# A graph layer on one core: 20 rounds of four gathered units instead of 18 rounds of five

## What is computed

```python
h = x @ node_w.T
rf = edge_attr @ review_w.T
m = (h[src] + rf) * edge_weight
y = segment_sum(m, dst, num_segments=12500)
out = layernorm(x + y, axis=-1)
```

## Time and profile before

| | before |
|---|---|
| median of three runs | 2291.5 us |
| the profiled execution, its own time | 2279.48 us |
| its span | 2277.7 us |
| PE busy, share of the span | 1891.5 us, 83% |
| DVE busy | 1986.1 us, 87% |
| ACT busy | 962.4 us, 42% |
| POOL busy | 1674.5 us, 74% |
| granted TensorE clock, mean | 0.915 |

### The profile page before, as it was taken

How to read it: one execution, slowest core, us unless ns; L and a number is a source line. 1 busy time by engine, 2 the same in 40 slices (tenths; PEclk the granted TensorE clock), 3 DMA queues, 4 the chain that set the end, 5 groups by cost and what they waited for, 6 DMA issues and landing times.

```text
span 2277.7 us, 93210 instructions
## 1 busy us (share of the span) xinstructions
PE 1891.5 (83%) x35999; PEld 1641.8 (72%) x36000; DVE 1986.1 (87%) x6206; ACT 962.4 (42%) x1602; POOL 1674.5 (74%) x1539
## 2 busy tenths in 40 slices
PE   1659788979897989898998899789988998989974
PEld 1557677767776777777777778677777877877864
DVE  3969898989898989898998899889988998989974
ACT  0324344444344444444443445344434443444434
POOL 3777777777777777777777777777777777777700
PEclk8679998999898999999998999899988998989997
DMA  6224333433333333333333333333433333433302
GB/s 139 55 59 86 72 79 79 83 72 83 78 74 76 84 77 84 76 84 77 84 76 76 76 85 80 75 72 84 84 75 69 82 79 71 84 73 72 66 3 57
DMA packets 480104, 173.08 MB, mean 76 GB/s; under 512 B 443549, under 2 KB 455397, under 8 KB 479445
## 3 DMA queue, kind: packets, MB, share of 16 engines
q1 hardware_dynamic: 426791, 111.57, 22.8%
q0 software_dynamic: 49632, 51.95, 11.4%
q10 hardware_dynamic: 3218, 3.20, 0.7%
HBM read 163.39 MB, written 3.20 MB: 73 GB/s over the span
## 4 chain that ended last, share of the span: by engine, by line
POOL 67%; issue 20%; DVE 7%; PE 2%; DMA 1%; ACT 1%; DVEq 0%; POOLq 0%; ACTq 0%; SPq 0%
POOL rows L534 64%; DVE hot_lo L855 3%; DVE hot_key L854 2%; DMA counts<-dst 1%; POOL run_src L560 1%; POOL run_dst L560 1%; POOL run_w L560 1%; POOL dst_row L552 1%; PE x_ps L1438 1%; ACT x_tab L1308 1%; DMA dst_row<-dst,row_i 0%; PE count_ps L1425 0%; DVE packed L990 0%; PE count_ps L1451 0%; DVE x_tab L1010 0%
## 5 line engine op out<-in xcount | busy, mean ns | idle before, releaser
L534 POOL DMA_INDIRECT rows<-x,g_src_cols x1440 | 1584.3, 1100 | 443.6 <-issue 438.7
L1240 ACT ACTIVATE counts<-count_ps 128x588 f32<-128x588 f32 (+1 forms) x1192 | 851.9, 750 | 1138.3 <-PE count_ps L1425 1127.5
L1425 PE MATMUL count_ps<-hot_key,hot_lo 128*128 128x294 f32 x4552 | 897.9, 330 | 257.2 <-DVE hot_lo L855 213.0
L855 DVE SCALAR_TENSOR_TENSOR hot_lo<-count,cols 128x256 fp32r<-128x256 f16 x2276 | 1078.6, 474 | 0.0
L1425 PEld LDWEIGHTS count_ps<-hot_key,hot_lo 128*128 128x128 f32 x4552 | 673.6, 196 | 386.7 <-DVE hot_lo L855 247.5
L854 DVE TENSOR_SCALAR hot_key<-count,cols 128x294 fp32r<-128x294 f16 x2276 | 864.5, 380 | 47.8 <-PE count_ps L1425 27.7
L1438 PE MATMUL x_ps<-counts,x_tab 128*64 128x63 f32 x21364 | 800.2, 229 | 41.3 <-DVE sums L772 41.2
L1438 PEld LDWEIGHTS x_ps<-counts,x_tab 128*64 128x64 f32 x21364 | 725.6, 142 | 102.5 <-DVE sums L772 48.0
L1352 PE MATMUL unit_ps<-rows,g_hot 128*32 128x64 f32 x5760 | 120.8, 246 | 0.0
L1352 PEld LDWEIGHTS unit_ps<-rows,g_hot 128*32 128x32 f32 x5760 | 104.4, 127 | 18.2 <-issue 18.2
L802 DVE TENSOR_SCALAR off<-dst_row,b_all 126x128 f32<-126x128 int32 x18 | 5.2, 290 | 116.4 <-DMA dst_row<-dst,row_i 116.4
(11 more groups left out here) (196 smaller groups left out, 728.3 us busy)
## 6 DMA issues: line engine op xcount, KB each, us to landing
rows<-edge_attr SPq DMA_DIRECT2D x196, 512.0 KB
rows<-x,g_src_cols POOLq DMA_INDIRECT x1440
out<-x_tab SPq DMA_DIRECT2D x12, 256.0 KB
counts<-dst SPq DMA_DIRECT2D x1, 848.0 KB
a_stage<-dst SPq DMA_DIRECT2D x17, 48.0 KB
a_stage_w<-edge_weight SPq DMA_DIRECT2D x17, 48.0 KB
g_stage<-src SPq DMA_DIRECT2D x18, 40.0 KB
g_stage<-dst SPq DMA_DIRECT2D x18, 40.0 KB
```

What stands on the lines that cost most here:

```text
L534: pool.indirect_dma_start(out=g_x[:, i, t, :], out_offset=None, in_=x, in_offset=bass.IndirectOffsetOnAxis(ap=g_src_cols[at.p][:, k:k + 1] ...
L855: dve.scalar_tensor_tensor(hot_lo[h][:, :, :], count16[:, 0:P].unsqueeze(1).to_broadcast([P, 2, P]), cols_[:, LO, j:j + 1], cols_[:, W_LOW ...
L1240: act.activation(to, count_ps[(g + e) % 2][:, 0:n, 0:KEYS].rearrange("p a (h d) -> p a h d", d=D), ACT.Copy).then_inc(counts_read, 1)
L1425: done = pe.matmul(count_ps[(g + e) % 2][:, k % 2, 0:KEYS], hot_lo[h][:, i, :], hot_key[h][:, :], start=(i == 0), stop=(i == 1))
```

## The change

Two constants. All sizes that follow from them change too: 80 gathered units instead of 90, 20 x 378 = 7560 counted nodes instead of 6804, 116 attribute units instead of 106 (of which the last round has two), `rows` with one unit of 4 KB per partition less, and `a_dst` with 116 partitions instead of 106.

```diff
-ROUNDS = 18
-GATHERED = 5
+ROUNDS = 20
+GATHERED = 4
```

## The result

The kernel after takes 2341.32 us in the median of four runs (2336.34 to 2343.08), the kernel before 2289.68 in the runs beside them: 1.0226 times as long, 95% interval 1.0195 to 1.0257. Slower, as forecast. The forecast was 2370, 29 us too high, and the range of 2340 to 2410 holds the time only at its edge, by 1.3 us.

The account below looks back on a forecast made before the run. POOL, saturated by 84 DMAs a round (117.7 us), was taken as the bound, DVE as the next. Two more rounds +115.0, start -31.5, end -4.5 gave +79 us, 2358.5, put on the median as 2370; range 2340 to 2410.

Parts of the forecast that it names:

- POOL's saturation and its end: POOL's DMA queue in the rounds: 84 DMAs, 117.7 us, become 68, 95.3 us; POOL then waits and L802's wait goes.
- What is late next is DVE itself: At L802 in the rounds: the wait goes and DVE sets the pace; POOL's saving beyond 5.6 us a round is worthless.
- DVE per round: DVE's work in a round: 112.1 us left to itself, less 1.1 for the fifth unit, gives 111.0 us.
- The branch, 7.6 us: Loop's branch back, in step 0: 25.2 us with it, 17.6 without; 8 in 18 rounds, the same share as before.
- Rival 2: Steps 4 and 5: PE becomes the bound at its lower clock, 57 us more, 2427 us; chance 14%.
- Rival 1: Rounds: DVE runs faster once not stopped, through L854, branches and slow last steps; 106.6 us a round, 2291 us; chance 5%.
- slow last steps: Part of rival 1: last steps of 18.0 us instead of 16.2, four in 16 rounds, 0.5 us a round, vanish.
- POOL's waits: POOL in the rounds: waits for DVE's row numbers (step 0) and run numbers (end of step 1), together 12 to 17 us.
- The start: Up to the second L802: -31.5 us, 145.76 to 114.3, with -10.2 from a faster a_dst load and fewer gathers ahead.
- rival 3: Start: the a_dst load isn't spread over more engines, L1043 at 27 us, 2382 us; chance 12%.
- The end: After the last L802: -4.5 us from missing fifth units and fewer attribute units in the last round; the tail doesn't change.
- The base: Profile against median: the profiled 2279.5 us lay 12 us below the median, so 2358.5 was lifted to 2370.

Follow-up runs that it names:

- the relief: Kernel before, 18 rounds and five units, with the fifth unit's 16 gathers issued in round 0 only and its other work kept: 2171.66 us, 0.949 times before.
- the renewed load: Kernel after with 16 spare gathers a round into a buffer nobody reads: 2546.03 us, 1.1121 times before.
- the branch experiment: Four rounds in the loop's body instead of two: in the kernel after 2316.43 us, 1.0115 times before; in the kernel before 2289.59 us, 0.9999.
- the run with spare gathers: Kernel after with 16 more gathers a round into a spare buffer nobody reads: 2546.03 us, 1.1121 times before.
- the first experiment: Kernel before with the fifth unit's 16 gathers issued in round 0 only, all other work kept: 2171.66 us, 0.949 times before.
- 90 in the last: 19-round kernel of five and four units in turn, load split, with the fifth unit fetched in its own round behind the next row: 2252.71 us, 0.9834 times before.

## Why the prediction was right, and what was off

**POOL's saturation and its end: right.** No wait at L802 in the rounds, a chain led by DVE, POOL with time left. Both halves show it, the relief (0.949) and the renewed load (1.112), and so does the branch experiment. One word of the prediction is too strong: GpSimd does compute in the set-up (L662, 5.5 us); in the rounds it only issues DMAs.

**"What is late next is DVE itself": right.** DVE is busy for 95.5% of the stretch (forecast: over 93%).

**DVE per round: mis-sized by 0.86 us, 18 x 0.86 = 15.5 us of the 29.** The term that failed is the 112.1 us that "DVE, left to itself, would need". The sum took out the wait at L802 and kept every other idle time and every duration. The run with the fifth unit not fetched measures it: with POOL relieved and DVE's work unchanged a round takes 111.14 us. Of the 1.0 us between, 0.75 is idle time that stood in no row under L802's name (per round, DVE idled 179.9 / 16 = 11.24 us before, 5.57 of it at L802 and 5.67 elsewhere; in that run 4.92 elsewhere), and 0.24 is busy time (106.46 to 106.21). The largest piece of the idle time is the wait for `count_ps` at L854, which fell from 24.7 us to 18.6. The fifth unit's work, forecast at 1.12 us, is 1.0 (111.14 to 110.15), which takes the error back to 0.86.

Why the other waits shrank stays open. It's tempting to call them an echo of the stall: DVE stops, PE runs out of work, the granted clock falls (0.93 in the stretch before, 0.97 with POOL relieved, 0.96 in the kernel after), and DVE waits for the slower PE in turn. But the run with spare gathers speaks against this as a rule. There the stall is back, 177.0 / 18 = 9.8 us a round, and the clock is down to 0.92, yet DVE's idle time elsewhere is (256.4 - 177.0) / 18 = 4.4 us a round, less than the 5.0 of the kernel after, and its waits for `count_ps` are 14.6 us, less than 16.2. The round grew by 9.5 us, 0.3 less than the wait at the row.

**The branch, 7.6 us: right**, and it stayed. DVE's timeline of the kernel after, the ends of steps 5 to 0 and of one whole round; the branch is before the second row:

```profile
1185.12 0.47 DVE L772 TENSOR_TENSOR sums<-sums,x_ps 64x63 f32 x2
1210.10 0.47 DVE L772 TENSOR_TENSOR sums<-sums,x_ps 64x63 f32 x2
1229.16 0.47 DVE L772 TENSOR_TENSOR sums<-sums,x_ps 64x63 f32 x2
1247.24 0.47 DVE L772 TENSOR_TENSOR sums<-sums,x_ps 64x63 f32 x2
1264.58 0.47 DVE L772 TENSOR_TENSOR sums<-sums,x_ps 64x63 f32 x2
1282.83 0.47 DVE L772 TENSOR_TENSOR sums<-sums,x_ps 64x63 f32 x2
1299.03 0.47 DVE L772 TENSOR_TENSOR sums<-sums,x_ps 64x63 f32 x2
1316.66 0.47 DVE L772 TENSOR_TENSOR sums<-sums,x_ps 64x63 f32 x2
```

Step 0 takes 25.0 us with the branch and 17.6 without, as in the earlier trace rows. Step 5 takes 16.2. With five branches fewer, the rounds gave back 6.9 us for each.

**Rival 2, PE as the bound in steps 4 and 5: did not come.** Step 4, without its fifth unit, is 18.2 us, and step 5 is 16.2 in the rows above where the earlier trace rows has a case of 18.0; such cases are gone. The wait that I had read as the cause is still there, in PE's timeline:

```profile
1389.98 1.52 PE L1438 MATMUL x_ps<-counts,x_tab 128*64 128x63 f32 x38 [1.32 <-DVE sums L772]
```

The same 1.32 us as in the earlier trace rows, but the 38 pieces take 1.52 us and not 2.40. So this wait by itself doesn't bring the clock down to 0.50. What does stays open. The stall at L802 isn't shown to: the slow piece begins some 60 us behind it, and the run with spare gathers stops at its row in every round and has no step 5 over 16.9 us.

**Rival 1, a faster DVE: one of its three parts came, at two thirds of its price.** The slow last steps went. The prediction counted four of them in 16 rounds; three lie there (they begin at 1731.77, 1851.51 and 1970.96 us) and the fourth behind, at 2090.23, so they had cost 3 x 1.8 / 16 = 0.34 us a round and not 0.5. L854 didn't move: 863.8 us for 2268 is 0.381, as 767.2 for 2016 was, though a fifth of the DMAs had gone. The branch didn't move.

**POOL's waits: the place was wrong.** I had said 12 to 17 us a round at the row numbers and the run numbers. It is 12.5 in the mean at unit 0 of the next round, for L706; the row is waited for three times in all (21.0 us), the runs hardly, since by then POOL has been held up already. POOL's timeline of the kernel after:

```profile
1199.86 1.09 POOL L552 DMA_INDIRECT dst_row<-dst,row_i  x1 [0.30 <-issue]
...
1218.34 1.01 POOL L534 DMA_INDIRECT rows<-x,g_src_cols  x1 [17.39 <-DVE g_src_cols L706]
```

The time didn't hang on it, but the design does: with 19 rounds, giving POOL something to do in this wait was worth 48 us (2300.26 to 2252.71).

**The start: -27.0 instead of -31.5.** DVE's part of 10.2 was put at L1043 at 15 us; it stands at 18.69, 6.8 earlier. The step that failed is the load's duration: the chain in order of time has

```profile
2.72 15.95 DMA counts<-dst
```

where 29 x 0.44 gave 12.7. The other 0.7 us were lost behind it, where the wider arrays cost 1.1 us and not 0.4: DVE reaches the second row 5.7 us earlier, not 6.8. That the load went onto more engines than before was right (rival 3 asked for 27 us), and so was the rule of the Trainium skill that stood behind it ("DMA: Bandwidth & Descriptors", "Why a DMA increments its semaphore by 16 and not by 1"). This case's traces agree with it: of the 8 KB packets at the start, one per partition of such a load, 1.9 run at a time in the kernel before from 12 us on, and 3.7 in the kernel after (from 12 to 16.7 us). What failed is the constant price of 0.44 us a partition. In both kernels such a packet takes 0.51 to 0.58 us in the mean up to 12 us, while the other loads of the start run, and 0.31 to 0.34 from 15 us on. 0.44 was the mean over a load with more than half of its time after 12 us; most of the shorter load falls before that, and 15.95 / 29 is 0.55.

**The end: -10.5 instead of -4.5.** The steps behind the last L802 lost 8.2, the tail 2.3. The last round lost 3.9, near the 3.3 that were forecast for it. The five steps ahead of it lost 4.3 where 1.1 was forecast: step 2 went from 19.3 to 17.9 us and step 5 from 18.0 to 16.0. Both went with POOL's load alone: with the fifth unit not fetched they're 17.9 and 16.7. The tail "doesn't change" was wrong by one gap, DVE's line ahead of the last products, in the kernel before and in the kernel after:

```profile
2224.32 0.69 DVE L998 SCALAR_TENSOR_TENSOR x_tab<-packed,x_tab 128x512 f32<-128x512 f32 x1 [3.98 <-issue]
```

```profile
2286.39 0.69 DVE L998 SCALAR_TENSOR_TENSOR x_tab<-packed,x_tab 128x512 f32<-128x512 f32 x1 [1.55 <-issue]
```

DVE waits there for nothing that the profile shows, so the cause of the 2.4 us stays open.

**The base.** On the profiled executions the change is +62.3 us, on the medians +51.6. The forecast lifted the profiled sum by the 12 us by which the profile of before lay under its median; the profile of after lay at its median, 2341.78 to 2341.32. So of the 29 us, 12 are base (2358.5 against 2370), and 17 are the sum (+79 against +62): -15.5, +4.5 and -6.0.

**The range held by 1.3 us, and that was luck in part.** Its low end was added up from four savings: a faster L854 (6.5 us), the whole wait at the start (6.9), the slow last steps (9) and cheaper branches (7). Of these only the slow last steps came, at 18 x 0.34 = 6 us. L854 and the branches didn't move, and the start gave back 4.5 us less and not 6.9 more. What brought the time down to the low end was other: the 12 us of base, the rest of DVE's waits besides L802, and the end.

## What to carry to other kernels

When a saturated helper engine is relieved, the gain is bounded by the second engine, here at 111 of 117.7 us a round, so work that is added to pay for the relief must be priced at that engine's rate and not at the helper's. Look for the middle before trading everything: two engines that are both nearly full beat either extreme, but only where each round's dependences let the helper spend its idle time (the same 86 units took 2300 us and 2253 us, by their place in one queue). Don't take a stall's row for its whole price: removing 5.6 us a round at L802 gave 6.6, and adding 9.8 elsewhere cost 9.5. Such a term wants a margin to both sides until a run has measured it.

## What the hardware showed beyond that

- **Gathers of one shape differ from kernel to kernel.** The median is 1.04 us, but the mean goes from 1.045 (fifth unit not fetched) over 1.096 (before) and 1.13 (after) to 1.157 and 1.169, by a few dozen that take 2 to 9 us: 80 over 1.5 us before, 48 after, 24 in the first experiment, 90 in the last. It costs only where POOL has no slack. What makes them long stays open.
- **The number of partitions moved the start behind a load** from 25.5 us (106) over 18.7 (116) to 9.5 (110) and 9.1 (96 + 10). With 116 it varied with the run: 18.7, 20.3 and 21.6 us for the same load in three kernels.
- **POOL's DMAs slow some of DVE's instructions, and not the ones that cost most.** L854 takes 0.381 us at 84 DMAs a round and at 68; the 0.364 of the earlier trace rows came where no gather ran at all. But L744, six times a round, moves with the load: the first line is the kernel before, the second the run with the fifth unit not fetched, in their 16 rounds.

```profile
L744 DVE TENSOR_SCALAR a_slot_hot<-column,a_slot_dst 128x128 f32<-128x128 f32 x96 | 36.8, 384 | 3.0
L746 DVE TENSOR_SCALAR a_slot_hot<-column,a_slot_dst 128x128 f32<-128x128 f32 x96 | 31.8, 332 | 3.1
```

  It is 0.372 us in the kernel after and 0.419 with spare gathers. L737 goes the same way: 0.293, 0.280, 0.280 and 0.310. In a round all this is about 0.3 us.
- **TensorE kept its upper level better once DVE didn't stop**: a mean granted clock of 0.96 and 0.97 in the rounds against 0.93, and 0.92 when the spare gathers brought the stop back. DVE's waits for `count_ps` don't follow it: 16.2 us in 18 rounds at 0.96 and 14.6 at 0.92.
